# Cross-attention stages L2 and L3: value blocks ahead of the masked scores, the bias row in the first tile's step, key bias and exp table first

## The chip, the cores and the metric

The kernel is one program on one core of a Trainium2 chip. The core has five engines with one instruction stream each: PE (TensorE, matrix products and transposes), DVE (VectorE), ACT (ScalarE), POOL (GpSimd) and SP, which here only issues transfers. Each engine works through its own stream in order and waits at semaphores. ACT also issues transfers from its stream. The time is that of one execution on the device in microseconds, and lower is better.

## The reference

An input `x` of 4 x 1024 x 256 goes through four layers. Each layer adds a gated cross-attention to a short context (4 x 77 x 256) and then a gated feed-forward block. The change concerns the attentions of the third and fourth layer (L2 and L3 in the names), which one function builds. Both are ordinary softmax attentions with 16 heads of 16; L2 has an additive mask and no biases, L3 a key mask and biases on q, k, v and the output.

```python
q = (x_q @ Wq.T).reshape(b, tq, h, hd).transpose(0, 2, 1, 3)
k = (x_kv @ Wk.T).reshape(b, tk, h, hd).transpose(0, 2, 1, 3)
v = (x_kv @ Wv.T).reshape(b, tk, h, hd).transpose(0, 2, 1, 3)
scores = jnp.einsum('bhqd,bhkd->bhqk', q, k) / jnp.sqrt(jnp.float32(hd))
scores = scores + attn_mask
...
w = jax.nn.softmax(scores, axis=-1)
out = jnp.einsum('bhqk,bhkd->bhqd', w, v)
...
x = x + jnp.tanh(g_xattn[2]) * _L2_xattn_ref(_layernorm(x, axis=-1), ctx_1024, ...)
x = x + jnp.tanh(g_xattn[3]) * _L3_xattn_ref(_layernorm(x, axis=-1), ctx_1024, ctx_1024, ...)
```

## The kernel before

The program is eight stages in a row, one for each attention and each feed-forward block. A barrier of all engines closes every stage, so nothing of the next one, its transfers included, starts earlier. `x` stays in the on-chip memory (`all_x`) as 32 tiles of 128 rows by 256; 8 tiles belong to one batch element.

`stage_mha` builds the L2 attention (names `l2x_...`) and the L3 attention (`l3x_...`). The context part comes first: PE projects the 4 x 77 context rows with `wk` into `score` (`project`, L2078), ACT copies the result to `kt` with the key bias `bk` (L2210), and DVE multiplies `kt` with the head mask `hm` into block-diagonal keys `kbd` (`key_block`, L1926). Values go the same way: `project` with `wv` into `p_bank`, ACT copy to `vt` (L2231), DVE `value_block` into `vbd` (L1955), then PE turns `vbd` (`first_values`, L2089), and ACT copies it to `vrow` (L2222). For the output bias PE multiplies `bvb` (the value bias, spread over 128 columns, L1951) with `wo` (`out_bias`, L2119), and DVE makes the row `brow` from it in two instructions (L1995, L1996).

A tile t then runs through: DVE `norm` (`xn`, L170); PE `turn` (L2126); ACT `copy_x`; PE `query` (L2135); ACT `copy_q` (`qt`, L2252); PE `scores` (L2148); DVE `masked_scores` (L2013), and for each half of the heads a maximum and a subtraction (`shift`, L2022 and L2024); ACT `exps` (L2264); PE `values`, which transposes the probabilities (L2164), while ACT copies them to `pt` (`copy_p`, L2272), and multiplies them with `vrow` (L2179); DVE `scale_o` (L2030, L2033); PE `turn_o` and `output` (L2193); DVE `update` of `x` and its statistics.

`unrolled(n, parts)` writes the order of every engine out: in step s, each part in the list handles tile s + lead, if there is one. The order in the list is the order in the stream. So a list entry that does something for tile 0 alone (`first_keys`, `first_values`, `out_bias`, `values_projection`) stands at one fixed place, in the step -lead. In `values`, the product with `vrow` waits for `v_ready` (all of `vrow`) and, in tile 0, for `brow_ready`, because the bias product stands in the same `o_bank` until DVE has read it. The Vector stream first waits for one semaphore, `bias_loaded`, up to 64, so for all four bias transfers, before it scales `bk`.

## Time and profile before

| | us |
|---|---|
| median of 3 runs | 2046.88 |
| lowest and highest of the 3 | 2042.46, 2048.35 |
| the profiled execution, its own time | 2042.43 |
| its span in the profile | 2040.7 |
| L2 attention, from its first transfer to the next stage's | 872.95 to 1135.24 |
| L3 attention, its first transfer | 1561.14 |

The profile's span covers nearly the whole execution: 1.7 us lie around it. Of the busy time PE has 1697.1 us (83% of the span), DVE 1152.6 (56%), ACT 887.5 (43%) and POOL 325.0 (16%). The rows further down give a start in us from the span's start, a duration, the engine and the line; a bracket at the end is the time that the engine sat idle before it, and who ended that.

### The profile page before, as it was taken

How to read it: one execution, taken by the hardware profiler on the slowest of the kernel's cores; microseconds unless marked ns; L12 is line 12 of the kernel's file. 1: busy time of each engine (PE TensorE's matmuls, PEld its weight loads, DVE VectorE, ACT ScalarE, POOL GpSimd, SP SyncE). 2: the span in 40 equal slices, each digit the busy share in tenths (PEclk: the TensorE clock that was granted, in tenths of full speed). 3: DMA queues.
4: the chain of work that ended last, by engine and by line, in shares of the span. 5: the costliest groups of instructions: out<-in, count | busy, mean ns of one | idle time of the engine just before them, and what ended most of it. 6: DMA issues, size and time to landing. Idle time of an engine off the chain costs nothing. (4 is left out here: it accounts for less than half of the span.)

```text
span 2040.7 us, 30775 instructions
## 1 busy us (share of the span) xinstructions
PE 1697.1 (83%) x10297; PEld 1295.8 (63%) x10297; DVE 1152.6 (56%) x2517; ACT 887.5 (43%) x1828; POOL 325.0 (16%) x362
## 2 busy tenths in 40 slices
PE   6888478888669999779999839999982899969998
PEld 4444234555456666558888729999971788855446
DVE  4544546776534556769998472322227798861115
ACT  2222356766343220236665235565543566633223
POOL 1000000000000000411110044555545111101110
PEclk8888789999789999889999659999996999989999
DMA  4000100000300000010000751222225000010002
...
DMA packets 63458, 78.53 MB, mean 38 GB/s; under 512 B 13999, under 2 KB 53195, under 8 KB 62936
## 3 DMA queue, kind: packets, MB, share of 16 engines
...
## 5 line engine op out<-in xcount | busy, mean ns | idle before, releaser
L2635 PEld LDWEIGHTS moe_bank<-moe_xt,moe_w1e 128*128 128x128 f32 x1264 | 155.0, 194 | 5.9 <-DVE moe_xt L2493 1.9
L2635 PE MATMUL moe_bank<-moe_xt,moe_w1e 128*128 128x128 f32 x1264 | 155.8, 277 | 1.1 <-DVE moe_xt L2493 1.1
L2645 PE MATMUL moe_bank<-moe_w,moe_xin 128*128 x632 | 149.3, 379 | 0.0
L2696 ACT ACTIVATE moe_xin<-moe_bank,moe_b 128x128 f32<-128x128 f32 x316 | 90.3, 368 | 125.1 <-PE moe_bank L2635 125.1
L356 PE MATMUL l0f_hb<-l0f_xt,l0f_w 128*128 128x512 f32 x256 | 123.5, 613 | 5.6 <-DVE l0f_a L287 3.9
L935 POOL TENSOR_TENSOR all_x<-all_x,l1f_bias 128x256 f32 x32 | 23.1, 726 | 647.6 <-DVE l1f_xn L170 647.6
L2645 PEld LDWEIGHTS moe_bank<-moe_w,moe_xin 128*128 128x128 f32 x632 | 114.0, 190 | 12.3
L175 DVE BATCH_NORM_STATS2 all_stats<-all_x 128x6 f32<-128x256 f32 (+1 forms) x256 | 105.8, 422 | 15.3 <-DMA all_x<-in_x 2.9
L2502 DVE TENSOR_TENSOR moe_y<-moe_bank,moe_b2r 128x256 f32<-128x256 f32 x79 | 33.5, 424 | 118.8 <-PE moe_bank L2645 118.8
L2562 POOL DMA_INDIRECT moe_results<-moe_y,moe_row x79 | 78.1, 989 | 125.0 <-DVE moe_y L2502 121.7
L2493 DVE COPY moe_xt<-moe_bank 128x256 f32<-128x256 f32 x79 | 33.5, 425 | 106.7 <-PE moe_bank L2623 106.7
L1749 PE MATMUL l3f_bank<-l3f_xt,l3f_wx 128*128 128x512 f32 x192 | 86.4, 600 | 0.0
L2687 ACT ACTIVATE moe_w1e<-moe_w 128x1024 f32 x79 | 83.5, 1058 | 3.3 <-issue 1.5
L2179 PE MATMUL l2x_o_bank<-l2x_vrow,l2x_pt 128*128 128x136 f32 (+1 forms) x640 | 82.3, 284 | 2.9 <-DVE l2x_brow L1996 2.9
L2179 PE MATMUL l3x_o_bank<-l3x_vrow,l3x_pt 128*128 128x136 f32 (+1 forms) x640 | 82.3, 284 | 2.9 <-DVE l3x_brow L1996 2.9
L1824 ACT ACTIVATE l3f_gate<-l3f_bank,l3f_bg 128x512 f32<-128x512 f32 x48 | 32.9, 687 | 115.1 <-PE l3f_bank L1757 105.4
L2557 POOL DMA_INDIRECT moe_xin<-moe_inputs,moe_token x79 | 76.9, 974 | 26.3 <-PE moe_bank L2623 21.6
L2179 PEld LDWEIGHTS l2x_o_bank<-l2x_vrow,l2x_pt 128*128 128x128 f32 (+1 forms) x640 | 78.1, 193 | 3.6 <-issue 3.1
L2179 PEld LDWEIGHTS l3x_o_bank<-l3x_vrow,l3x_pt 128*128 128x128 f32 (+1 forms) x640 | 78.1, 193 | 3.6 <-issue 3.1
L285 DVE SCALAR_TENSOR_TENSOR l0f_a<-l0f_hb,l0f_cw,l0f_a 128x1023 f32<-128x1023 f32 x32 | 41.0, 1283 | 61.5 <-ACT l0f_a L467 61.5
L356 PEld LDWEIGHTS l0f_hb<-l0f_xt,l0f_w 128*128 128x128 f32 x256 | 45.8, 196 | 46.9 <-issue 45.9
L1757 PE MATMUL l3f_bank<-l3f_ct,l3f_wc 128*128 128x512 f32 x144 | 63.8, 592 | 0.0
...
## 6 DMA issues: line engine op xcount, KB each, us to landing
...
```

Source lines behind the costliest of these rows:

```text
L175: return nc.vector.bn_stats(sh.stats[:, ds(t * 6, 6)], x_tile(sh, t))
L285: k.link(nc.vector.scalar_tensor_tensor(a[:, u, 1:S], h[:, 0:S - 1], cw[:, m, 0:1], a[:, u, 1:S], ALU.mult, ALU.add))
L356: ins = nc.tensor.matmul(hb[g % 2][:, half * 512:(half + 1) * 512], w1[:, d, m * P:(m + 1) * P], xt[:, b % 2, d, half * 512:(half + 1) * 5 ...
L1749: ins = nc.tensor.matmul(bank[3 * m + k][:, :], wx[:, k, c, m * P:(m + 1) * P], xt[:, c, b * S + j * G:b * S + (j + 1) * G], start=(c == 0 ...
L1757: ins = nc.tensor.matmul(bank[3 * m + k][:, :], wc[:, k, c, m * P:(m + 1) * P], ct[:, b % 2, c, j * G:(j + 1) * G], start=False, stop=(c = ...
L2179: ins = nc.tensor.matmul(o_bank[:, m * VW:(m + 1) * VW], pt[0:rows(i), u, n, j * P:(j + 1) * P], vrow[0:rows(i), ds((t // TB) * (DC * NV * ...
L2557: nc.gpsimd.indirect_dma_start(out=gathered(t), out_offset=None, in_=xnd, in_offset=bass.IndirectOffsetOnAxis(ap=token[:, t:t + 1], axis=0 ...
L2562: nc.gpsimd.indirect_dma_start(out=ys, out_offset=bass.IndirectOffsetOnAxis(ap=row[:, t:t + 1], axis=0), in_=y[:, u, :], in_offset=None).t ...
L2635: ins = nc.tensor.matmul(out, w1e[:, at:at + P], xt[:, u, c * P:(c + 1) * P], start=(c == 0), stop=(c == DC - 1))
L2645: ins = nc.tensor.matmul(bank[4 + u][:, 0:D], ht[:, u, c * P:(c + 1) * P], w2[:, ds(e * (HC * D) + c * D, D)], start=(c == 0), stop=(c == ...
L2687: nc.scalar.activation(w1e[:, u * DC * HID:(u + 1) * DC * HID], w1[:, ds(e * (DC * HID), DC * HID)], ACT.Copy).then_inc(s.w1e_ready, 1)
L2696: ins = nc.scalar.activation(ht[:, u, m * P:(m + 1) * P], bank[1 + u][:, m * P:(m + 1) * P], ACT.Gelu, bias=b1[:, ds(e * HC + m, 1)])
```

## The change

`unrolled` gets another order in three lists. On DVE `first_values` now stands ahead of `masked_scores`, and `out_bias` has lead 2 in place of 1, so it comes in the step in which tile 0 gets its scores, one step earlier. On PE `out_bias` and `first_values` change places. On ACT `first_values` comes ahead of both `exps`. The copy to `bvb` moves behind the first keys and the mask. The transfers that ACT issues get another order, with a semaphore of their own for the key bias (`bk_loaded`) and for the output bias (`bo_loaded`): key bias, head mask, `wv`, query and value bias, `wo`, output bias. A new activation with Exp on one column (`warm`) follows them, whose result nobody reads.

```diff
--- before.py
+++ after.py
@@ -1889,6 +1889,7 @@
         vbd = s.sb("vbd", [P, 2, DC, HW_])
         vrow = s.sb("vrow", [P, B * DC * NV * VW])
         ones_row = s.sb("ones_row", [P, NV, HH])
+        warm = s.sb("warm", [P, 1])
         keyrow = s.sb("keyrow", [P, B, SK], U8)
         mraw = s.sb("mraw", [P, TB, SK], U8 if masked else F32)
         mask_t = s.sb("mask_t", [P, T, SK])
@@ -1904,7 +1905,7 @@
         x_bank, o_bank = s.ps("x_bank", [P, 512]), s.ps("o_bank", [P, 512])
         score = s.ps("score", [P, NG, 512])
         p_bank = [s.ps(f"p_bank{k}", [P, 512]) for k in range(2)]
-        sems = ["wk_loaded", "wv_loaded", "wq_loaded", "wo_loaded", "hm_loaded", "bias_loaded", "small_loaded", "kv_ps", "kv_ready", "vbd_ready", "kbd_ready", "kbd_rest_ready", "v_ps", "v_ready", "brow_ps",
+        sems = ["wk_loaded", "wv_loaded", "wq_loaded", "wo_loaded", "hm_loaded", "bk_loaded", "bias_loaded", "bo_loaded", "small_loaded", "kv_ps", "kv_ready", "vbd_ready", "kbd_ready", "kbd_rest_ready", "v_ps", "v_ready", "brow_ps",
                 "brow_ready", "bvb_ready", "bk_ready", "set_step", "mask_set", "xn_ready", "xt_ps", "xt_ready", "q_ps", "q_ready",
                 "s_ps", "added", "max_ready", "shifted", "exp_ready", "ones_set", "inv_ready", "pt_ps", "pt_ready",
                 "o_ps", "o_ready", "ot_ps", "ot_ready", "y_ps", "biased", "x_ready", "stats_ready"]
@@ -1942,13 +1943,12 @@
             def _(dve):
                 c = norm_vector(nc, dve, sh, s)
                 if bias_names:
-                    dve.wait_ge(s.bias_loaded, 64)
+                    dve.wait_ge(s.bk_loaded, 16)
                 else:
                     for a in (bq, bk, bv):
                         c.link(nc.vector.memset(a[:, :], 0.0))
                     c.link(nc.vector.memset(brow[:, :], 0.0))
                 nc.vector.tensor_scalar(bk[:, :], bk[:, :], HD ** -0.5, None, ALU.mult).then_inc(s.bk_ready, 1)
-                nc.vector.tensor_copy(bvb[:, :, :], bv[:, :].unsqueeze(2).to_broadcast((P, DC, P))).then_inc(s.bvb_ready, 1)
                 hmb = hm[:, :].unsqueeze(2).to_broadcast((P, HH, SK))
 
                 def value_block(b, k):
@@ -1972,6 +1972,9 @@
                             key_block(nc.vector, 0, k, s.kbd_ready)
                         dve.wait_ge(s.small_loaded, smalls)
                         mask_block(0)
+                        if bias_names:
+                            dve.wait_ge(s.bias_loaded, 32)
+                        nc.vector.tensor_copy(bvb[:, :, :], bv[:, :].unsqueeze(2).to_broadcast((P, DC, P))).then_inc(s.bvb_ready, 1)
 
                 def first_values(t, u):
                     if t == 0:
@@ -1991,6 +1994,8 @@
                 def out_bias(t, u):
                     if t:
                         return
+                    if bias_names:
+                        dve.wait_ge(s.bo_loaded, 16)
                     dve.wait_ge(s.brow_ps, 1)
                     c.link(nc.vector.tensor_tensor(brow[:, :], o_bank[:, 0:D], brow[:, :], ALU.add))
                     nc.vector.tensor_scalar(brow[:, :], brow[:, :], tg, None, ALU.mult).then_inc(s.brow_ready, 1)
@@ -2042,8 +2047,8 @@
                     dve.wait_ge(s.x_ready, ev(t))
                     tile_stats(nc, sh, t).then_inc(s.stats_ready, 1)
 
-                unrolled(T, [(scale_o, 0), (norm, 4), (first_keys, 3), (masked_scores, 2), (shift(0), 2), (update, 0), (shift(1), 2), (first_values, 2),
-                             (out_bias, 1), (context, 0)])
+                unrolled(T, [(scale_o, 0), (norm, 4), (first_keys, 3), (first_values, 2), (masked_scores, 2), (shift(0), 2), (update, 0), (shift(1), 2),
+                             (out_bias, 2), (context, 0)])
                 dve.wait_ge(s.stats_ready, T)
 
             @block.gpsimd
@@ -2193,17 +2198,21 @@
                         ins = nc.tensor.matmul(o_bank[:, 0:D], ot[:, u, k * P:(k + 1) * P], wo[:, k, :], start=(k == 0), stop=(k == DC - 1))
                     ins.then_inc(s.y_ps, 1)
 
-                unrolled(T, [(turn, 3), (scores, 2), (turn_o, 0), (query, 3), (output, 0), (values_projection, 3), (first_values, 2), (out_bias, 2), (values, 1), (context, 0)])
+                unrolled(T, [(turn, 3), (scores, 2), (turn_o, 0), (query, 3), (output, 0), (values_projection, 3), (out_bias, 2), (first_values, 2), (values, 1), (context, 0)])
 
             @block.scalar
             def _(act):
+                if bias_names:
+                    act.dma_start(bk[:, :], io[bias_names[1]]).then_inc(s.bk_loaded, 16)
                 act.dma_start(hm[:, :], io.head_mask).then_inc(s.hm_loaded, 16)
+                act.dma_start(wv[:, :, :], weight_view(io[wv_T])).then_inc(s.wv_loaded, 16)
                 if bias_names:
-                    for a, n in zip((bq, bk, bv), bias_names):
+                    for a, n in ((bq, bias_names[0]), (bv, bias_names[2])):
                         act.dma_start(a[:, :], io[n]).then_inc(s.bias_loaded, 16)
-                    act.dma_start(brow[:, :], io[bias_names[3]].partition_broadcast(P)).then_inc(s.bias_loaded, 16)
-                act.dma_start(wv[:, :, :], weight_view(io[wv_T])).then_inc(s.wv_loaded, 16)
                 act.dma_start(wo[:, :, :], weight_view(io[wo_T])).then_inc(s.wo_loaded, 16)
+                if bias_names:
+                    act.dma_start(brow[:, :], io[bias_names[3]].partition_broadcast(P)).then_inc(s.bo_loaded, 16)
+                nc.scalar.activation(warm[:, :], sh.gates[:, 0:1], ACT.Exp)
                 act.wait_ge(s.bk_ready, 1)
                 for j in range(DC):
                     act.wait_ge(s.kv_ps, j + 1)
@@ -2246,6 +2255,8 @@
                     nc.scalar.activation(xt[:, u, :], x_bank[:, 0:D], ACT.Copy).then_inc(s.xt_ready, 1)
 
                 def copy_q(t, u):
+                    if t == 0 and bias_names:
+                        act.wait_ge(s.bias_loaded, 32)
                     act.wait_ge(s.q_ps, ev(t))
                     act.wait_ge(s.s_ps, ev(t, back=2))
                     for m in range(DC):
@@ -2271,7 +2282,7 @@
                         act.wait_ge(s.pt_ps, ev(t, NB, n + 1))
                         nc.scalar.activation(pt[0:r, u, n, 0:k * P], p_bank[n % 2][0:r, 0:k * P], ACT.Copy).then_inc(s.pt_ready, 1)
 
-                unrolled(T, [(copy_x, 3), (copy_o, 0), (copy_q, 3), (values_projection, 3), (copy_p, 1), (exps(0), 2), (exps(1), 2), (first_values, 2), (context, 0)])
+                unrolled(T, [(copy_x, 3), (copy_o, 0), (copy_q, 3), (values_projection, 3), (copy_p, 1), (first_values, 2), (exps(0), 2), (exps(1), 2), (context, 0)])
 
 
 def stage_l2_xattn(nc, io, sh):
```

On PE in the L3 attention (L2 reads alike), from the query of tile 1 on, to the product with `vrow` in tile 0. The first fence is before, the second the same place after the change.

```order
L2135 MATMUL l3x_x_bank<-l3x_xt,l3x_wq 128x128 x4
L2089 MATMUL l3x_p_bank<-all_ident,l3x_vbd 128x128 x8
L2089 MATMUL l3x_p_bank<-all_ident,l3x_vbd 104x128 x2
L2119 MATMUL l3x_o_bank<-l3x_wo,l3x_bvb 128x256 x2
L2126 MATMUL l3x_x_bank<-all_ident,l3x_xn 128x128 x2
L2148 MATMUL l3x_score<-l3x_kbd,l3x_qt 128x154 x8
L2135 MATMUL l3x_x_bank<-l3x_xt,l3x_wq 128x128 x4
L2164 MATMUL l3x_p_bank<-all_ident,l3x_pr 128x128 x8
```

```order
L2140 MATMUL l3x_x_bank<-l3x_xt,l3x_wq 128x128 x4
L2124 MATMUL l3x_o_bank<-l3x_wo,l3x_bvb 128x256 x2
L2094 MATMUL l3x_p_bank<-all_ident,l3x_vbd 128x128 x8
L2094 MATMUL l3x_p_bank<-all_ident,l3x_vbd 104x128 x2
L2131 MATMUL l3x_x_bank<-all_ident,l3x_xn 128x128 x2
L2153 MATMUL l3x_score<-l3x_kbd,l3x_qt 128x154 x8
L2140 MATMUL l3x_x_bank<-l3x_xt,l3x_wq 128x128 x4
L2169 MATMUL l3x_p_bank<-all_ident,l3x_pr 128x128 x8
```

The bias product (`l3x_o_bank<-l3x_wo,l3x_bvb`) went from behind the transposes of `vbd` to ahead of them. The number of instructions is the same.

On DVE in the L3 attention, from the first keys on, before and after; `l3x_vbd` are the value blocks, `l3x_pr` the masked scores.

```order
L170 TENSOR_SCALAR l3x_xn<-all_x,all_rstd,all_shift 128x256
L2013 TENSOR_TENSOR l3x_pr<-l3x_score,l3x_mask_t 128x616 x2
L2022 TENSOR_REDUCE l3x_mx<-l3x_pr 128x8
L2024 TENSOR_TENSOR l3x_pr<-l3x_pr,l3x_mx 128x616
L2022 TENSOR_REDUCE l3x_mx<-l3x_pr 128x8
L2024 TENSOR_TENSOR l3x_pr<-l3x_pr,l3x_mx 128x616
L1955 TENSOR_TENSOR l3x_vbd<-l3x_vt,l3x_hm 128x616 x2
L170 TENSOR_SCALAR l3x_xn<-all_x,all_rstd,all_shift 128x256
L2013 TENSOR_TENSOR l3x_pr<-l3x_score,l3x_mask_t 128x616 x2
L2022 TENSOR_REDUCE l3x_mx<-l3x_pr 128x8
L2024 TENSOR_TENSOR l3x_pr<-l3x_pr,l3x_mx 128x616
L2022 TENSOR_REDUCE l3x_mx<-l3x_pr 128x8
```

```order
L170 TENSOR_SCALAR l3x_xn<-all_x,all_rstd,all_shift 128x256
L1955 TENSOR_TENSOR l3x_vbd<-l3x_vt,l3x_hm 128x616 x2
L2018 TENSOR_TENSOR l3x_pr<-l3x_score,l3x_mask_t 128x616 x2
L2027 TENSOR_REDUCE l3x_mx<-l3x_pr 128x8
L2029 TENSOR_TENSOR l3x_pr<-l3x_pr,l3x_mx 128x616
L2027 TENSOR_REDUCE l3x_mx<-l3x_pr 128x8
L2029 TENSOR_TENSOR l3x_pr<-l3x_pr,l3x_mx 128x616
L2000 TENSOR_TENSOR l3x_brow<-l3x_o_bank,l3x_brow 128x256
L2001 TENSOR_SCALAR l3x_brow<-l3x_brow,all_gates 128x256
L170 TENSOR_SCALAR l3x_xn<-all_x,all_rstd,all_shift 128x256
L2018 TENSOR_TENSOR l3x_pr<-l3x_score,l3x_mask_t 128x616 x2
L2027 TENSOR_REDUCE l3x_mx<-l3x_pr 128x8
```

The two value blocks moved ahead of the first masked scores, and `brow`, which before followed the second tile's subtractions, now stands between the first tile's and the second tile's.

On ACT at the start of the L3 attention, before and after.

```order
L2200 DMA l3x_hm<-in_head_mask 128x8
L2203 DMA l3x_bq<-in_L_xattn_b_q_cols 128x2
L2203 DMA l3x_bk<-in_L_xattn_b_k_cols 128x2
L2203 DMA l3x_bv<-in_L_xattn_b_v_cols 128x2
L2204 DMA l3x_brow<-in_L_xattn_b_o 128x256
L2205 DMA l3x_wv<-in_L_xattn_W_v_T 128x2x256
L2206 DMA l3x_wo<-in_L_xattn_W_o_T 128x2x256
L2210 ACTIVATE l3x_kt<-l3x_score,l3x_bk 128x308 x2
L2246 ACTIVATE l3x_xt<-l3x_x_bank 128x256
L2252 ACTIVATE l3x_qt<-l3x_x_bank,l3x_bq 128x128 x2
L2231 ACTIVATE l3x_vt<-l3x_p_bank 128x308 x2
```

```order
L2206 DMA l3x_bk<-in_L_xattn_b_k_cols 128x2
L2207 DMA l3x_hm<-in_head_mask 128x8
L2208 DMA l3x_wv<-in_L_xattn_W_v_T 128x2x256
L2211 DMA l3x_bq<-in_L_xattn_b_q_cols 128x2
L2211 DMA l3x_bv<-in_L_xattn_b_v_cols 128x2
L2212 DMA l3x_wo<-in_L_xattn_W_o_T 128x2x256
L2214 DMA l3x_brow<-in_L_xattn_b_o 128x256
L2215 ACT_TABLE_LOAD
L2215 ACTIVATE l3x_warm<-all_gates 128x1
L2219 ACTIVATE l3x_kt<-l3x_score,l3x_bk 128x308 x2
L2255 ACTIVATE l3x_xt<-l3x_x_bank 128x256
```

The key bias is the first transfer in place of the third, `wv` the third in place of the sixth, the output bias the last. The table load, which before stood ahead of the first exps, comes with `warm` ahead of the first `kt` copy.

## Rows read from the trace of the kernel before

**Rows 1.** Busy time by stretch: PE, PEld, DVE, ACT, POOL, then PEclk, DMA share, GB/s

```profile
884.00:896.00 12.00, 6.91 (x44) 5.24 (x42) 6.25 (x9) 4.67 (x10) 0.00 (x0) 0.73 0.00 1
...
920.00:950.00 30.00, 28.39 (x264) 25.58 (x264) 27.59 (x48) 18.43 (x40) 4.09 (x5) 1.00 0.01 1
```

**Rows 2.** Timeline of the L2 attention, its first tile

```profile
884.37 0.43 ACT L2231 ACTIVATE l2x_vt<-l2x_p_bank 128x308 f32<-128x308 f32 x1 [0.61 <-PE l2x_p_bank L2078]
885.22 1.16 PE L2135 MATMUL l2x_x_bank<-l2x_xt,l2x_wq 128*128 128x128 f32 x8
885.42 1.51 DVE L2013 TENSOR_TENSOR l2x_pr<-l2x_score,l2x_mask_t 128x616 f32<-128x616 f32 x2 [2.22 <-PE l2x_score L2148]
...
889.20 0.80 DVE L2024 TENSOR_TENSOR l2x_pr<-l2x_pr,l2x_mx 128x616 f32<-128x616 f32 x1
889.92 1.50 DVE L1955 TENSOR_TENSOR l2x_vbd<-l2x_vt,l2x_hm 128x616 f32<-128x616 f32 x2
...
891.47 2.56 PE L2089 MATMUL l2x_p_bank<-all_ident,l2x_vbd 128*128 128x128 f32 x10 [5.09 <-DVE l2x_vbd L1955]
892.63 0.69 ACT L2222 ACTIVATE l2x_vrow<-l2x_p_bank,all_gates 128x512 f32<-128x512 f32 x1 [1.88 <-PE l2x_p_bank L2089]
...
893.48 1.22 ACT L2222 ACTIVATE l2x_vrow<-l2x_p_bank,all_gates 128x512 f32<-128x512 f32 x3 [0.17 <-PE l2x_p_bank L2089]
...
895.54 0.63 PE L2126 MATMUL l2x_x_bank<-all_ident,l2x_xn 128*128 128x128 f32 x2
...
897.14 1.51 DVE L2013 TENSOR_TENSOR l2x_pr<-l2x_score,l2x_mask_t 128x616 f32<-128x616 f32 x2 [5.40 <-PE l2x_score L2148]
...
901.64 0.42 DVE L1995 TENSOR_TENSOR l2x_brow<-l2x_o_bank,l2x_brow 128x256 f32<-128x256 f32 x1
...
902.70 4.22 PE L2179 MATMUL l2x_o_bank<-l2x_vrow,l2x_pt 128*128 128x136 f32 x20 [2.92 <-DVE l2x_brow L1996]
...
906.96 0.26 DVE L2030 RECIPROCAL l2x_ri<-l2x_o_bank 128x16 f32<-128x16 f32 x1 [4.51 <-PE l2x_o_bank L2179]
```

**Rows 3.** Timeline of the L2 attention: durations and distances at the full clock

```profile
896.93 1.16 PE L2135 MATMUL l2x_x_bank<-l2x_xt,l2x_wq 128*128 128x128 f32 x8
...
897.92 1.04 PE L2164 MATMUL l2x_p_bank<-all_ident,l2x_pr 128*128 128x128 f32 x8
...
898.64 1.56 ACT L2272 ACTIVATE l2x_pt<-l2x_p_bank 128x512 f32<-128x512 f32 x3
...
908.98 1.03 PE L2193 MATMUL l2x_o_bank<-l2x_wo,l2x_ot 128*128 128x256 f32 x4
...
911.52 2.52 PE L2179 MATMUL l2x_o_bank<-l2x_vrow,l2x_pt 128*128 128x136 f32 x20
```

**Rows 4.** Timeline, the L2 and then the L3 attention's start

```profile
880.22 0.41 PE L2126 MATMUL l2x_x_bank<-all_ident,l2x_xn 128*128 128x128 f32 x2 [0.28 <-ACTq L2213]
...
1564.06 4.48 PE L2078 MATMUL l3x_score<-all_ctx_t,l3x_wk 128*128 128x308 f32 x8 [43.55 <-DMA l3x_wk<-in_L_xattn_W_k_T]
...
1567.88 0.33 DVE L1950 TENSOR_SCALAR l3x_bk<-l3x_bk 128x2 f32<-128x2 f32 x1 [2.64 <-DMA l3x_brow<-in_L_xattn_b_o]
...
1568.24 0.93 ACT L2210 ACTIVATE l3x_kt<-l3x_score,l3x_bk 128x308 f32<-128x308 f32 x2 [17.66 <-DVE l3x_bk L1950]
...
1569.44 0.44 PE L2126 MATMUL l3x_x_bank<-all_ident,l3x_xn 128*128 128x128 f32 x2 [0.91 <-DVE l3x_xn L170]
...
1576.32 1.28 ACT L2264 ACT_TABLE_LOAD   x1
...
1577.75 0.72 ACT L2264 ACTIVATE l3x_pr<-l3x_pr 128x616 f32<-128x616 f32 x1 [0.15 <-DVE l3x_pr L2024]
```

**Rows 5.** DMA issues at the L3 start: KB each, median us to landing

```profile
l3x_wo<-in_L_xattn_W_o_T ACTq DMA_DIRECT2D x1, 256.0 KB, 4.9
...
l3x_bk<-in_L_xattn_b_k_cols ACTq DMA_DIRECT2D x1, 1.0 KB, 3.7
```

**Rows 6.** Timeline, DVE: the reciprocal of tile 1, L2

```profile
914.07 0.26 DVE L2030 RECIPROCAL l2x_ri<-l2x_o_bank 128x16 f32<-128x16 f32 x1 [0.69 <-PE l2x_o_bank L2179]
```

## The prediction

> **What bounds the kernel now.** I first read the busy time by stretch, to see whether the two attentions are full. In mid-stage they are: PE is busy 28.39 of 30 us and DVE 27.59, at the full clock of 2.4 GHz [rows 1]. Their first tile is not: PE has 6.91 of 12 us, and the mean granted clock is 0.73 of full, so about half of this stretch ran at 1.2 GHz. The timeline of the L2 attention says why [rows 2]. After the query of tile 1 ends at 886.38, PE stands at the transposes of the value blocks, 5.09 us, because DVE makes these blocks only after tile 0's masked scores, maxima and subtractions. Behind the transposes in PE's stream stand the bias product, the transposes of tile 2's `xn` (895.54) and the scores of tile 1, so DVE then waits 5.40 us for these scores. Last, PE waits 2.92 us for `brow`, which DVE makes after tile 1's subtractions, and DVE waits 4.51 us for the product with `vrow`, which runs at the low clock in 4.22 us. From there the pace is even: the reciprocals of tiles 0 and 1 start at 906.96 and 914.07, 7.11 us apart [rows 2, 6], and the engines keep to this cycle. What shifts the first reciprocal shifts the rest of the stage and, since barriers separate the stages, the end. That is the place where I read the change off: the start of tile 0's reciprocal, in each of the two stages.
>
> **L2, step by step.** The last `vt` copy ends at 884.37 + 0.43 = 884.80, and DVE, idle 2.22 us there, can start the value blocks at about 884.9 [rows 2]. They take 1.50 us (1.42 to the next start, 889.92 to 891.34 by the pair's own overlap), so the blocks are ready at 886.4 and tile 0's masked scores start at 886.3 instead of 885.42: 0.9 us later. From that start to the end of the last subtraction takes 889.20 + 0.80 - 885.42 = 4.58 us, which gives 890.9. `brow` is two instructions, the first of 0.42 us; the product that waits for both began 902.70 - 901.64 = 1.06 us after the first. I take 0.8, to 891.7, the next `xn` 0.4, so DVE is free for tile 1's masked scores at 892.1.
>
> PE: the query of tile 1 ends at 886.38 [rows 2]. The bias product follows at once; at the full clock its shape takes 1.03 us (the row of L2193, 908.98) [rows 3], with overlap to 887.3. The value blocks are ready, so their transposes start there. For the same ten transposes of probabilities ACT's copy starts 0.72 us after PE's (898.64 against 897.92) [rows 3]. ACT then copies `vrow` in 0.69 + 1.22 = 1.9 us [rows 2], 888.0 to 890.0. PE's transposes are done at 889.1, and tile 2's turn and tile 1's scores, which took no more than 897.14 - 895.54 = 1.6 us at partly the low clock, at about 890.2. So tile 1's masked scores start when DVE is free, 892.1, not 897.14, and its last subtraction ends at 896.7.
>
> ACT: the exps now stand behind the `vrow` copies. The first, whose subtraction is done at about 889.3, waits to 890.0 for them; the second starts at 890.9, when its subtraction is done, and ends at 891.6. Behind it stands the copy of tile 2's `xt`, which the query of tile 2 waits for: query at 892.1. From query to the transposes is 0.99 us, from there to the last of the copies to `pt` 2.3 us (898.64 + 1.56 - 897.92), but in the even cycle the product starts 1.7 us after the transposes, so I put it at 2.7 us after the query, 894.8 [rows 3]. `brow` is ready three us before, so that wait is gone. With the product at the full clock, 2.52 us [rows 3], the reciprocal starts at 897.4: 906.96 - 897.4 = 9.6 us gained.
>
> **L3** has the same rows 688.7 to 689.4 us later, so the same 9.6, and three edits more. DVE there waits 2.64 us for the last of the four bias transfers, the copy to `bvb` follows, and tile 0's first turn starts at 1569.44, 0.90 us after the projection's end at 1564.06 + 4.48 = 1568.54. In L2, where no bias is loaded, PE idled 0.28 us there [rows 4]. The key bias landed 3.7 us after its issue [rows 5]; issued first, at about 1561.15, it is there at 1564.9, before DVE's norm is done (1567.88 - 2.64 = 1565.24), and PE's projection, which it doesn't need, is the bound: gain 0.6, taken as 0.5 because `wv` now loads beside `wk`. The bounds of this edit are 0 and 0.6 us. Second, the Exp table load, 1.28 us [rows 4]. Before it lay under DVE's maxima (after the load, ACT still idled 0.15 us for DVE's subtraction before the first exps at 1577.75), so its removal there gives nothing; its new place is under PE's projection, where ACT idled 17.66 us. In L2 `warm` falls under the projection as well; without that cover it would cost less than the 0.43 us of a copy of 308 columns [rows 2], and in L3 1.28 more. Third, `wo`, which PE now wants ahead of the value transposes, and behind which the whole PE stream would stand: it is needed at about 1575 and, issued near 1563.7 with 4.9 us to landing [rows 5], there at 1569. The output bias is issued behind it and used on DVE near 1580. Nothing for both.
>
> **The clock.** The sum so far is 9.6 + 9.6 + 0.5 = 19.7 us. It presupposes PE at 2.4 GHz, and the new order leaves an idle gap: from 890.2 to 892.1, 1.9 us. In the rows the clock fell after PE idled 5.09 us and again after 2.92 us, where the product took 4.22 us in place of 2.52; in the even cycle it stays, with 30 - 28.39 = 1.6 us of idling over four tiles, so 0.4 us for each [rows 1 to 3]. A gap of 1.9 lies between 0.4 and 2.92, nearer to 2.92 (1.0 against 1.5), so I take the low clock for one stretch: 4.22 - 2.52 = 1.7 us, in each stage. The bounds are 0 and, with the transposes slow as well (ten in 2.56 us against eight in 1.04, so 1.3 for ten), 2.9. The Trainium skill, "TensorE: Matmul & The Clock Gate", section "Why this matters for your kernels", asks for no idle gaps over about 3 us between bursts; by this rule alone the gap of 1.9 us would cost nothing and the sum would be 19.7. The row of 2.92 us, just under that figure, shows a fall, so the rule is not sharp enough here.
>
> **Sum.** 19.7 - 3.4 = 16.3 us off the profiled execution's 2042.4: 2026.1. That execution is as fast as the fastest of the three runs; the median lies 4.4 above. I put the expected median 2 us above the sum: 2028. A measurement of this kernel tells 0.3%, some 6 us, from no change.
>
> **Rivals.** *The clock holds* (0.27): the gap is short enough, as the skill's rule has it. Full 19.7 us, 2022.7; for it speaks that PE is busy nearly without a gap from 880 to 890, against it the fall after 2.92 us.
> *The first tile takes the gain back in part* (0.12): ACT's copies before the exps or the slow transposes delay tile 0 more than I count, and both stages lose 2.9 us to the clock, so that with 2 us of such delay about 5 us each remain: 2042.4 - 10 = 2032. For it: ACT's exps do wait 0.7 us. Against: DVE is the later one in the sum.
> *It is hidden anyway* (0.04): tile 1 gains, but the even cycle is reached at the old time, because something outside these rows sets it (the x update, POOL). 2042. Against it: the rows show no such wait, and POOL is nearly idle.
> *Slower* (0.02): PE falls to the low clock in the new gap and, with DVE now feeding it sooner but in small pieces, stays there. At the low clock the product costs 1.7 and the transposes 1.2 us more per tile; from four tiles on (4 x 2.9 = 11.6 us in a stage) the gain of 9.6 is gone, and at seven in each stage it is 2 x (20.3 - 9.6) = 21 us slower: 2063. Against it: after each fall in the rows a tile of solid work brought the full clock back.
> My forecast, the low clock for one stretch in each stage, has 0.55.
>
> **Numbers.** The two first cases span 2022.7 to 2026.1 for a run like the profiled one, up to 2033 with the 4.4 us of the median and the third case 2032 to 2036. The range 2020 to 2035 leaves out the last two cases, part of the third, and a tail below. Faster by over 0.3%: the first three cases, 0.94; within: 0.04; slower: 0.02.
>
> **What would show it.** In the changed profile, in L2: value blocks on DVE from about 884.9, the bias product on PE right after the query at 886.4, PE's 5.09 us wait and DVE's 5.40 us wait gone, tile 1's masked scores near 892.1, tile 0's reciprocal near 897 to 899, and then 7.11 us between reciprocals as before. In L3: the scaling of `bk` right behind the norm, the table load under the projection. PEclk in the second twelve us tells forecast from rival. The prediction is wrong if DVE waits for PE's scores of tile 1 again, if the product with `vrow` still waits for `brow`, or if the later distance between tiles grows.

## The result and the profile after

| | before | changed |
|---|---|---|
| median, us | 2047.22 (4 runs, 2042.46 to 2048.35) | 2029.75 (4 runs, 2027.91 to 2032.66) |
| ratio | | 0.992, 95% interval 0.9899 to 0.9942 |
| profiled execution, us | 2042.43 | 2031.57 |
| L2 attention, first transfer to the next stage's | 262.29 | 253.78 |
| L3 attention, the same | 263.34 | 254.08 |
| the six other stages together | 1515.07 | 1521.94 |

The change is faster by 17.5 us of the medians, well over the 6 us that a measurement tells; forecast were 2028 us and a range of 2020 to 2035. The two attentions gave 8.51 + 9.26 = 17.77 us. The two profiled executions differ by only 10.9 us, because the six stages that the change does not touch took 6.9 us longer in the second one. Of these, 2.65 us lie in the stage between the two attentions, and that part comes with the change (next section). The page of the changed kernel has the shorter span and nearly the same busy times as before: the gain is idle time.

```profile
span 2029.8 us, 30778 instructions
...
PE 1697.8 (84%) x10297; PEld 1296.2 (64%) x10297; DVE 1153.8 (57%) x2517; ACT 887.8 (44%) x1830; POOL 325.4 (16%) x362
```

The stage lengths come from the first transfer of each stage, since a barrier stands ahead of it. These are those of the changed kernel, from its timeline of issues: 1130.00 - 876.22 = 253.78 for L2, 1812.63 - 1558.55 = 254.08 for L3.

```profile
876.22 0.38 SPq L1933 DMA_DIRECT2D l2x_wk<-in_L_xattn_Wk_T  x1
...
1130.00 0.37 SPq L2386 DMA_DIRECT2D moe_wr<-in_L_ffn_Wr  x1
...
1558.55 0.37 SPq L1933 DMA_DIRECT2D l3x_wk<-in_L_xattn_W_k_T  x1
...
1812.63 0.37 SPq L1637 DMA_DIRECT2D l3f_wx<-in_L_ffn_wf_T  x1
```

The L2 attention's first tile in the changed kernel, its timeline, to be read against [rows 2] (the stage began 3.27 us later in this execution, so subtract that):

```profile
888.08 1.51 DVE L1955 TENSOR_TENSOR l2x_vbd<-l2x_vt,l2x_hm 128x616 f32<-128x616 f32 x2 [1.23 <-ACT l2x_vt L2240]
...
889.46 1.03 PE L2124 MATMUL l2x_o_bank<-l2x_wo,l2x_bvb 128*128 128x256 f32 x4
889.50 1.50 DVE L2018 TENSOR_TENSOR l2x_pr<-l2x_score,l2x_mask_t 128x616 f32<-128x616 f32 x2
...
890.33 1.04 PE L2094 MATMUL l2x_p_bank<-all_ident,l2x_vbd 128*128 128x128 f32 x8
...
894.00 0.42 DVE L2000 TENSOR_TENSOR l2x_brow<-l2x_o_bank,l2x_brow 128x256 f32<-128x256 f32 x1
...
895.04 1.50 DVE L2018 TENSOR_TENSOR l2x_pr<-l2x_score,l2x_mask_t 128x616 f32<-128x616 f32 x2
895.15 1.17 PE L2140 MATMUL l2x_x_bank<-l2x_xt,l2x_wq 128*128 128x128 f32 x8 [2.07 <-ACT l2x_xt L2255]
...
896.15 2.50 PE L2169 MATMUL l2x_p_bank<-all_ident,l2x_pr 128*128 128x128 f32 x10
...
898.45 3.07 PE L2184 MATMUL l2x_o_bank<-l2x_vrow,l2x_pt 128*128 128x136 f32 x20
...
901.55 0.26 DVE L2035 RECIPROCAL l2x_ri<-l2x_o_bank 128x16 f32<-128x16 f32 x1 [1.58 <-PE l2x_o_bank L2184]
...
908.66 0.26 DVE L2035 RECIPROCAL l2x_ri<-l2x_o_bank 128x16 f32<-128x16 f32 x1 [0.69 <-PE l2x_o_bank L2184]
```

PE's wait of 5.09 us for the value blocks, DVE's of 5.40 us for the scores and PE's of 2.92 us for `brow` are gone: the masked scores of tile 1 and the product with `vrow` carry no bracket. New is PE's gap of 2.07 us ahead of the query of tile 2, which waits for ACT's copy to `xt`. The ten transposes behind it take 2.50 us, as at the low clock. The reciprocals of tiles 0 and 1 are 7.11 us apart, as in [rows 2, 6].

The table of busy times, with columns as in [rows 1]; the first number behind POOL's is PEclk, the granted clock as a share of 2.4 GHz:

```profile
887.27:899.27 12.00, 9.59 (x82) 7.91 (x81) 11.02 (x17) 7.16 (x17) 2.88 (x4) 0.87 0.01 1
...
923.27:953.27 30.00, 28.39 (x273) 25.27 (x271) 26.22 (x47) 18.82 (x41) 4.09 (x5) 1.00 0.01 1
...
894.00:896.00 2.00, 0.84 (x7) 0.85 (x8) 1.97 (x6) 0.99 (x2) 1.12 (x2) 1.00 0.00 0
896.00:899.00 3.00, 3.00 (x16) 2.56 (x16) 2.97 (x4) 2.13 (x6) 1.77 (x3) 0.53 0.00 0
```

In the 12 us that answer to the first row of [rows 1], PE is busy 9.59 us in place of 6.91 and DVE 11.02 in place of 6.25. The even cycle is unchanged (PE 28.39 of 30 both times). The clock falls right behind the gap: 1.00, then 0.53 (nearly all at 1.2 GHz).

### The profile page after: what moved, and what is told of

The parts are those of the page before. It is cut to its first block and busy times, and to the rows that moved or that the text cites. A ratio compares the mean times of both kernels' runs of the same rounds, so it can differ in the third digit from the quotient of the medians.

```text
span 2029.8 us, 30778 instructions
## 1 busy us (share of the span) xinstructions
PE 1697.8 (84%) x10297; PEld 1296.2 (64%) x10297; DVE 1153.8 (57%) x2517; ACT 887.8 (44%) x1830; POOL 325.4 (16%) x362
```

## The experiments

All times in this table run from the first transfer of the stage, so they can be compared between executions whose earlier stages differ. "Reciprocal" is the start of tile 0's, L2 then L3.

| kernel | median, us | ratio (95%) | L2 length | L3 length | reciprocal |
|---|---|---|---|---|---|
| before | 2047.22 | | 262.29 | 263.34 | 34.01, 35.19 |
| changed | 2029.75 | 0.992 (0.9899-0.9942) | 253.78 | 254.08 | 25.33, 25.85 |
| e1_orders | 2033.65 | 0.993 (0.9907-0.9953) | 253.74 | 257.24 | 25.40, 29.00 |
| e2_loads | 2046.11 | 0.9999 (0.9985-1.0012) | 262.33 | 263.31 | 33.98, 35.09 |
| e3_values_only | 2035.82 | 0.9945 (0.9924-0.9967) | 256.19 | 256.64 | 27.74, 28.40 |
| e4_brow_only | 2032.92 | 0.994 (0.9917-0.9963) | 256.70 | 256.97 | 28.35, 28.73 |
| e5_act_late | 2030.44 | 0.9926 (0.9906-0.9946) | 255.79 | 256.46 | 27.46, 28.21 |
| e6_x_early | 2026.21 | 0.9907 (0.9889-0.9924) | 252.26 | 252.53 | 23.64, 24.19 |
| e7_filler | 2024.16, one run | | 252.68 | 253.19 | 24.32, 24.93 |
| e8_orders_warm | 2031.53, one run | | 253.69 | 255.36 | 25.36, 27.14 |
| e9_no_warm | 2030.68, one run | | 253.55 | 254.36 | 25.21, 26.16 |
| e10_before_again | 2048.88, one run | | 262.34 | 263.29 | 34.03, 35.09 |
| e11_orders_again | 2031.67, one run | | 253.76 | 255.43 | 25.44, 27.23 |

The medians of the kernel before beside these were 2045.68 (e1 to e4) and 2046.20 (e5 to e8); one run of it beside e9 to e11 took 2040.42. The six other stages, which no kernel here touches, sum to 1515 us in one profiled execution of the kernel before and to 1521 in the other (e10). A few us between two medians can be that alone, so I read the stage lengths.

One of the six stages is not free of the change, though its code is. The MoE feed-forward between the two attentions, from its first transfer to that of L3, takes 428.2 to 429.1 us in five profiles (changed, e1, e8, e9, e11) and 425.7 to 426.6 in the eight others, those of the kernel before, e6 and e7 among them. The timelines of the two, at the same distance of 92.4 us into this stage, the kernel before first, then the changed kernel:

```profile
1227.66 2.05 PE L2635 MATMUL moe_bank<-moe_xt,moe_w1e 128*128 128x128 f32 x16 [0.52 <-DVE moe_xt L2493]
```

```profile
1222.44 3.78 PE L2646 MATMUL moe_bank<-moe_xt,moe_w1e 128*128 128x128 f32 x16 [0.52 <-DVE moe_xt L2504]
```

The same 16 products take 1.7 us more, since the clock rises to full later: its mean is 0.98 in the 6 us from 1227.24 before, and 0.56 in the 6 us from 1222.00 in the changed kernel. So some 2.6 us of the 17.77 are lost again behind L2. Why is not shown; a fall of the clock in L2 is not enough, since e3_values_only has one and takes 425.9 us here.

**e1_orders: the three new lists alone.** The kernel before with the orders of the change; transfers, the copy to `bvb` and the table load stay where they were.

```diff
# DVE
-... (first_keys, 3), (masked_scores, 2), ..., (shift(1), 2), (first_values, 2), (out_bias, 1), (context, 0)
+... (first_keys, 3), (first_values, 2), (masked_scores, 2), ..., (shift(1), 2), (out_bias, 2), (context, 0)
# PE
-... (first_values, 2), (out_bias, 2), (values, 1), (context, 0)
+... (out_bias, 2), (first_values, 2), (values, 1), (context, 0)
# ACT
-... (exps(0), 2), (exps(1), 2), (first_values, 2), (context, 0)
+... (first_values, 2), (exps(0), 2), (exps(1), 2), (context, 0)
```

> The three reordered lists alone; transfers, the wait for all four biases, the early copy to bvb and no warm activation, as before. Measure: from a stage's first transfer to tile 0's reciprocal, 34.0 us (L2) and 35.2 us (L3) before, 25.3 and 25.9 in the changed kernel. My theory (the orders are the whole gain of L2, and in L3 all but the late key bias and the exposed table load): L2 25.3; L3 25.9 + 0.5 for the key bias + 0.6, since the table load of 1.28 us now stands between the vrow copies and exps that DVE releases 0.7 us later, so about 27.0. Both stages together 16.5 us shorter than before. Rival (transfers and warm matter for more, as the table load is now fully on the path): L3 28 or later. Rival (they are worth nothing): L3 25.9.

L2 takes 253.74 us, as in the changed kernel (253.78): the orders are all of L2's gain. L3 takes 257.24, which is 3.16 us more than in the changed kernel; 1.1 were expected (27.0 against 25.9 to the reciprocal), and the prediction had 0.5 for the loads. The timeline of L3 in e1_orders:

```profile
1568.09 0.17 DVE L1950 TENSOR_SCALAR l3x_bk<-l3x_bk 128x2 f32<-128x2 f32 x1 [3.07 <-DMA l3x_brow<-in_L_xattn_b_o]
...
1569.66 0.44 PE L2126 MATMUL l3x_x_bank<-all_ident,l3x_xn 128*128 128x128 f32 x2 [1.87 <-DVE l3x_xn L170]
...
1570.57 2.08 PE L2135 MATMUL l3x_x_bank<-l3x_xt,l3x_wq 128*128 128x128 f32 x8 [0.47 <-ACT l3x_xt L2246]
...
1572.44 2.93 PE L2078 MATMUL l3x_p_bank<-all_ctx_t,l3x_wv 128*128 128x308 f32 x8
...
1580.60 1.28 ACT L2264 ACT_TABLE_LOAD   x1
```

DVE waits for the last of four bias transfers, and PE stands 1.87 us behind that. The query and the value projection behind this gap take 2.08 and 2.93 us, where the changed kernel has 1.16 and 2.24: PE runs at the low clock there (windows of e1_orders, PEclk 0.57).

```profile
1570.00:1574.00 4.00, 3.53 (x13) 2.97 (x13) 2.06 (x4) 1.01 (x3) 0.00 (x0) 0.57 0.00 0
```

The 3.16 us are there when the query of tile 2 starts (22.63 us into L3 against 19.47): 0.98 at the first turn (8.75 against 7.77), 1.58 from there to tile 0's masked scores (16.38 against 13.82), and 0.60 from these to the query, where the table load is now on ACT's path. Whether the 1.58 are the orders' doing or chance, e10 and e11 were made for.

**e2_loads: everything but the three lists.** The changed kernel with the old lists (the diff of e1_orders read backwards).

> The transfers' order, the wait for the key bias alone, the later copy to bvb and the warm activation; the three lists as before. My theory: L2 as before (34.0 us to the first reciprocal), L3 0.5 us earlier (34.7), total within noise of before. Rival (the loads carry a good part of the gain): more than 2 us in L3.

Ratio 0.9999; L3 263.31 against 263.34, and the first turn 8.29 us into the stage (before 8.30). The loads alone gave nothing in this profile, where 0.5 us had been expected in L3. The timelines of the L3 start show what they move, e2_loads first:

```profile
1569.26 0.37 SPq L1933 DMA_DIRECT2D l3x_wk<-in_L_xattn_W_k_T  x1
...
1572.65 4.34 PE L2083 MATMUL l3x_score<-all_ctx_t,l3x_wk 128*128 128x308 f32 x8 [44.09 <-DMA l3x_wk<-in_L_xattn_W_k_T]
...
1577.55 0.41 PE L2131 MATMUL l3x_x_bank<-all_ident,l3x_xn 128*128 128x128 f32 x2 [0.56 <-ACTq L2222]
```

and the changed kernel (its first transfer is at 1558.55, shown above):

```profile
1561.71 4.04 PE L2083 MATMUL l3x_score<-all_ctx_t,l3x_wk 128*128 128x308 f32 x8 [44.12 <-DMA l3x_wk<-in_L_xattn_W_k_T]
...
1562.19 1.28 ACT L2215 ACT_TABLE_LOAD   x1 [13.77 <-issue]
...
1566.32 0.41 PE L2131 MATMUL l3x_x_bank<-all_ident,l3x_xn 128*128 128x128 f32 x2 [0.57 <-ACTq L2222]
```

The wait for the biases has gone; PE idles 0.56 us at the turn in place of 0.91. On the other side `wk` lands later in the kernels that issue `wv` close behind it: the projection starts 3.39 us after the first transfer in e2_loads (1572.65 - 1569.26) and 3.16 in the changed kernel, before 2.92 (1564.06 - 1561.14 [rows 4]). The projection itself takes 3.8 to 4.5 us, as the clock happens to rise in it. So one profile doesn't settle a term of 0.5 us. Over all profiles it stands like this: with the new loads and the early table load (seven kernels) the first turn starts 7.73 to 8.29 us into L3, mean 7.93, and `wk` is there after 3.16 to 3.39; with the old transfers (five profiles) 8.30 to 8.75, mean 8.43, and 2.89 to 3.08. The loads bring the turn forward by 0.5 us in the mean, and e2_loads is the poorest of the seven.

**e3_values_only: value blocks first, bias row as before.**

```diff
 # DVE
-(out_bias, 2), (context, 0)
+(out_bias, 1), (context, 0)
 # PE
-(out_bias, 2), (first_values, 2)
+(first_values, 2), (out_bias, 2)
```

> As the changed kernel, but the bias product and its row stay where they were before (PE behind the value transposes, DVE behind tile 1's subtractions). My theory: PE's 5.1 us wait is gone, tile 1's masked scores start at about 18 us after the stage's first transfer, but the product with vrow then waits for the row, which DVE makes at about 22.6 to 23.4: first reciprocal at about 26.2 us (L2), so 7.8 us of the 8.7 gained. Rival A (the value blocks are all of it): 25.3, as in the changed kernel. Rival B (the row is the larger part): 29 or later.

L2 is 6.10 us shorter than before, L3 6.70. Tile 1's masked scores start 18.05 us into L2 in place of 24.19, so the earlier start of these scores, 6.14 us, is all of it. The reciprocal comes at 27.74, not at the 26.2 expected: the product still waits for `brow`, which DVE makes behind tile 1's subtractions, and it runs at the low clock, in 4.10 us, which the expectation had not counted. PE's query of tile 2 already stands 1.83 us for ACT's copy (timeline, L2):

```profile
898.99 1.16 PE L2140 MATMUL l2x_x_bank<-l2x_xt,l2x_wq 128*128 128x128 f32 x8 [1.83 <-ACT l2x_xt L2255]
...
902.65 0.42 DVE L2000 TENSOR_TENSOR l2x_brow<-l2x_o_bank,l2x_brow 128x256 f32<-128x256 f32 x1
...
903.71 4.10 PE L2184 MATMUL l2x_o_bank<-l2x_vrow,l2x_pt 128*128 128x136 f32 x20 [1.24 <-DVE l2x_brow L2001]
...
907.85 0.26 DVE L2035 RECIPROCAL l2x_ri<-l2x_o_bank 128x16 f32<-128x16 f32 x1 [4.39 <-PE l2x_o_bank L2184]
```

**e4_brow_only: bias row first, value blocks as before.**

```diff
 # DVE
-(first_values, 2), (masked_scores, 2), (shift(0), 2), (update, 0), (shift(1), 2), (out_bias, 2)
+(masked_scores, 2), (shift(0), 2), (update, 0), (shift(1), 2), (first_values, 2), (out_bias, 2)
 # ACT
-(first_values, 2), (exps(0), 2), (exps(1), 2)
+(exps(0), 2), (exps(1), 2), (first_values, 2)
```

> As the changed kernel, but the value blocks stay behind the first tile's subtractions on DVE, and the vrow copies behind the exps on ACT; only the bias product and its row are early. My theory: PE still waits about 4.2 us for the value blocks, tile 1's masked scores start near 22.4 us, the product no longer waits for the row: first reciprocal at 28 to 29.5 us in L2, 5.3 us gained, so that the two parts overlap (7.8 + 5.3 against 8.7). Rival (the parts add up): 34.0 - 0.9 = 33.1.

L2 is 5.59 us shorter than before, L3 6.37. PE still stands 4.23 us for the value blocks, and the product follows at the full clock, in 2.56 us and without a wait (timeline, L2):

```profile
889.81 2.56 PE L2094 MATMUL l2x_p_bank<-all_ident,l2x_vbd 128*128 128x128 f32 x10 [4.23 <-DVE l2x_vbd L1955]
...
897.00 2.56 PE L2184 MATMUL l2x_o_bank<-l2x_vrow,l2x_pt 128*128 128x136 f32 x20
```

The parts account for it: 2.92 us of wait for `brow` [rows 2], 4.22 - 2.56 = 1.66 us of clock in the product, and 24.19 - 23.03 = 1.16 us by which tile 1's masked scores come earlier, since the bias product no longer stands ahead of them in PE's stream: 5.7. Alone the two parts give 6.10 and 5.59 in L2; together they give 8.51, not 11.7. On top of e3_values_only the early row moves the reciprocal by 2.4 us (27.74 to 25.33) and not by 5.7, for three reasons. The wait for `brow` is 1.24 us there and not 2.92, since PE's query of tile 2 comes later than tile 1's masked scores, behind ACT's copy. The product goes from 4.10 to 3.07 us and not to 2.56, since the clock falls again in the full change (e7 below). And the 1.16 us in PE's stream are worth nothing where DVE is the later one: tile 1's masked scores carry no bracket in the changed kernel. That `brow` between the tiles delays these scores (18.82 against 18.05) costs nothing, since the query of tile 2 starts at 18.93 and 18.88.

**e5_act_late: ACT's list as before.** DVE and PE as changed, `first_values` behind both exps on ACT.

> As the changed kernel, but ACT copies vrow behind tile 0's exps, as before the change. My theory (ACT's place matters, since PE's last value transposes wait for the first of these copies, and tile 2's turn and tile 1's scores stand behind them): PE idles about 4 us, query of tile 2 at 20.9 us after the first transfer in place of 18.9, clock low, first reciprocal at 27.5 to 28.5 us in L2 (25.3 in the changed kernel), each stage 2 to 3 us longer. Rival (exps ahead help, because they gate tile 0): 25 or earlier.

L2 is 2.01 us longer than in the changed kernel, L3 2.38. The copies to `vrow` now stand behind exps that wait for DVE's second subtraction, PE stands 4.10 us in the middle of the value transposes, and tile 2's turn and tile 1's scores stand behind them (timeline, L2):

```profile
894.49 0.43 PE L2094 MATMUL l2x_p_bank<-all_ident,l2x_vbd 128*104 128x128 f32 x2 [4.10 <-ACT l2x_vrow L2231]
...
896.40 2.08 PE L2140 MATMUL l2x_x_bank<-l2x_xt,l2x_wq 128*128 128x128 f32 x8
```

So the third list is a part of the gain, and DVE's and PE's new places need it.

**e6_x_early: the copy to tile 2's `xt` between the two exps.** In the changed kernel this copy stands behind the second exp, and the query of tile 2 waits for it.

```diff
+                def next_x(t, u):
+                    if t == 0:
+                        copy_x(2, 0)
+
+                def later_x(t, u):
+                    if t != 2:
+                        copy_x(t, u)
+
-(copy_x, 3), ... (first_values, 2), (exps(0), 2), (exps(1), 2), (context, 0)
+(later_x, 3), ... (first_values, 2), (exps(0), 2), (next_x, 2), (exps(1), 2), (context, 0)
```

> As the changed kernel, but ACT's copy of tile 2's transposed xn stands between tile 0's two exps, where ACT idles 0.7 us for DVE, so that PE's query of tile 2 and the transposes behind it start 1.3 us earlier and PE's idle gap falls from 2.07 to about 0.8 us. My theory (the product of tile 0 waits for the chain exps, copy, query, transposes, and the gap lowers the clock): product at 20.6 at the full clock, first reciprocal at 23.4 to 23.5, now bounded by DVE's subtractions of tile 1; each stage 1.9 us shorter than in the changed kernel. Rival (DVE already bounds it): reciprocal no earlier than 25. Rival (the clock falls all the same): 24.3.

PE's gap shrinks from 2.07 to 0.64 us (timeline, L2), the clock stays (windows, PEclk 1.00 in the stretch behind it), and the product takes 2.56 us:

```profile
894.13 1.16 PE L2140 MATMUL l2x_x_bank<-l2x_xt,l2x_wq 128*128 128x128 f32 x8 [0.64 <-ACT l2x_xt L2255]
...
896.82 2.56 PE L2184 MATMUL l2x_o_bank<-l2x_vrow,l2x_pt 128*128 128x136 f32 x20
```

```profile
894.00:897.00 3.00, 2.44 (x19) 2.18 (x20) 2.96 (x7) 2.40 (x6) 1.71 (x3) 1.00 0.00 0
```

The reciprocal, at 23.64 where 23.4 to 23.5 was expected, carries no bracket, so DVE's own work bounds it now. The stages are 1.52 and 1.55 us shorter than in the changed kernel, where 1.9 was expected. The median is 3.5 us lower, the lowest of the kernels with more than one run; the MoE stage, 2.00 us shorter in this profile than in the changed one, may have a part in that. Against the kernel before it is 0.9907. The intervals of this ratio and the changed kernel's overlap; that it is the better of the two rests on the stage lengths.

**e7_filler: work for PE in the gap.** The bias product a second and third time, into a bank that is free then, ahead of the place where PE would stand. Nobody reads the result.

```diff
+                def filler(t, u):
+                    if t:
+                        return
+                    pe.wait_ge(s.v_ready, NB)
+                    for _ in range(2):
+                        for k in range(DC):
+                            nc.tensor.matmul(p_bank[1][:, 0:D], bvb[:, k, :], wo[:, k, :], start=(k == 0), stop=(k == DC - 1))
+
-(turn, 3), (scores, 2), (turn_o, 0), ...
+(turn, 3), (scores, 2), (filler, 1), (turn_o, 0), ...
```

> As the changed kernel, with two more bias products of PE into a bank that nobody reads then, placed in PE's idle gap between tile 1's scores and tile 2's query (extra work, no result used). My theory (the gap of 2.07 us lowers the clock): the gap is 0.2 us, PEclk stays at full, the product takes 2.52 us in place of 3.07 and the transposes before it 1.44 in place of 2.5, first reciprocal at 23.9 to 24.2 us in L2 (25.3). Rival (the fall has another cause): PEclk falls in the same place, 25.3 us or later.

The query of tile 2 starts at the same distance into L2 as in the changed kernel (19.03 us, 18.93 there), since it still waits for `xt`. But the clock is full behind it, and from query to reciprocal it takes 899.00 - 893.71 = 5.29 us in place of 901.55 - 895.15 = 6.40 (timeline and windows, L2):

```profile
893.71 1.16 PE L2140 MATMUL l2x_x_bank<-l2x_xt,l2x_wq 128*128 128x128 f32 x8
...
896.40 2.56 PE L2184 MATMUL l2x_o_bank<-l2x_vrow,l2x_pt 128*128 128x136 f32 x20
...
899.00 0.26 DVE L2035 RECIPROCAL l2x_ri<-l2x_o_bank 128x16 f32<-128x16 f32 x1 [0.47 <-PE l2x_o_bank L2184]
```

```profile
894.00:897.00 3.00, 2.58 (x23) 2.31 (x23) 2.96 (x5) 1.98 (x5) 2.34 (x4) 1.00 0.00 0
```

What differs is that PE works for 1.99 us where it had idled 2.07, and the clock stays full in both stages, as it does in both stages of e6_x_early. So it is PE's idling there that lowers the clock. The fall costs 1.1 us in L2 (253.78 - 252.68) and 0.9 in L3 by the stage lengths, and 1.1 in both from query to reciprocal.

**e8_orders_warm: e1_orders with the table load early.** It loads the table under the projection, as the change does, and leaves the transfers as before.

```diff
+                nc.scalar.activation(warm[:, :], sh.gates[:, 0:1], ACT.Exp)
                 act.wait_ge(s.bk_ready, 1)
```

> The three reordered lists and the warm activation, but the biases loaded and waited for as before. The orders alone gave 29.0 us to the first reciprocal in L3, the changed kernel 25.9: 3.1 us lie in the loads. My theory: 0.7 of them are the exposed table load, 0.6 to 1 the late turn of tile 0, and the rest PE at the low clock because it idled for the key bias. So here 28.3 if the clock falls at the start again, 26.6 if it does not. Rival (the table load is the whole loss): 25.9.

L3 takes 255.36 us, 1.88 less than e1_orders. From tile 0's masked scores to the query of tile 2 it takes 5.65 us in place of 6.25: 0.6 us are the load's. The reciprocal follows the query by 5.28 us in place of 6.37, so 1.1 are the clock's, which did not fall here behind the same gap of 2.07 us (timeline and windows, L3):

```profile
1579.55 1.16 PE L2136 MATMUL l3x_x_bank<-l3x_xt,l3x_wq 128*128 128x128 f32 x8 [2.07 <-ACT l3x_xt L2248]
...
1582.23 2.56 PE L2180 MATMUL l3x_o_bank<-l3x_vrow,l3x_pt 128*128 128x136 f32 x20
```

```profile
1578.00:1581.00 3.00, 1.46 (x13) 1.46 (x14) 2.96 (x7) 1.25 (x3) 1.73 (x3) 1.00 0.00 0
```

The reciprocal comes at 27.14, between the 28.3 expected with a fall at the start and the 26.6 without: the fall at the start came, the later one did not. The 1.28 us to the changed kernel are the later turn (8.45 against 7.77, 0.7 us) and again a low clock behind the wait for the biases (PE idles 1.28 us at the turn; the first query and the value projection take 1.27 and 3.85 us in place of 1.16 and 2.24, together 1.7), less the 1.1 us of clock that this execution saved at the query of tile 2.

**e9_no_warm: the changed kernel without `warm`.** The complement of e8: early transfers, late table load.

```diff
-                nc.scalar.activation(warm[:, :], sh.gates[:, 0:1], ACT.Exp)
```

> The changed kernel without the early table load; the complement of e8_orders_warm. If the late biases cost L3 through the clock (theory), the first query of L3 takes 1.16 us and its projection of values 2.24 us here as in the changed kernel, and only the load is exposed: L3 0.6 us longer than the changed kernel, 254.7. If orders and loads interact in another way (rival), L3 is 255.4 or more with the clock full at that place. L2 as changed, 253.7, or up to 0.6 more if its load is exposed too (the table of L2 may be loaded already).

L3 takes 254.36 us, only 0.3 more than the changed kernel. The timeline of L3 has both sides of the early load:

```profile
1565.14 0.41 PE L2130 MATMUL l3x_x_bank<-all_ident,l3x_xn 128*128 128x128 f32 x2 [0.28 <-ACTq L2220]
...
1577.47 1.69 PE L2139 MATMUL l3x_x_bank<-l3x_xt,l3x_wq 128*128 128x128 f32 x8 [2.67 <-ACT l3x_xt L2253]
```

Without it PE idles 0.28 us at the first turn, as in L2, and not 0.57; at the query of tile 2 it idles 2.67 us, and not 2.07. So the early load costs 0.3 us at the stage's start and saves 0.6 later. How it costs them stays open: ACT's `kt` copies start at the same distances in both (5.7 and 7.2 us), and what the turn waits for are ACT's semaphore increments, which stand behind them in the program. In L2, where `warm` runs but no table is loaded, the turn waits 0.28.

**e10_before_again and e11_orders_again: the kernel before and e1_orders once more.**

> The kernel before once more, to see whether the clock behind PE's wait for the biases in L3 (0.91 us there in its first profile, with the full clock behind it) falls in some executions of the same code. Theory, that it is chance of the execution: L3's first query at 1.2 to 2.1 us and the value projection up to 3.9 us in place of 2.24, stage up to 1.7 us longer than 263.34. Rival, that the old orders hold the clock there: query 1.16, projection 2.24, 263.3 again.

> The same code as e1_orders once more, where L3 took 257.24 with PE's gap of 1.87 us ahead of the first turn and a low clock behind it (query 2.08, value projection 2.93). Theory, that the fall there is chance: L3 between 255.5 (no fall) and 257.3 (fall). Rival, that the orders and the late biases together always cost it: 257.2 again.

The kernel before repeats itself, as the rival had it: L3 263.29, a gap of 0.84 us at the first turn, full clock behind it. e11 does not repeat e1: the same code takes 255.43 us in place of 257.24. The timeline of e11, L3:

```profile
1566.23 0.44 PE L2126 MATMUL l3x_x_bank<-all_ident,l3x_xn 128*128 128x128 f32 x2 [1.06 <-DVE l3x_xn L170]
...
1567.14 1.16 PE L2135 MATMUL l3x_x_bank<-l3x_xt,l3x_wq 128*128 128x128 f32 x8 [0.47 <-ACT l3x_xt L2246]
```

The gap is 1.06 us, the query takes 1.16. So the 1.6 us of e1's low clock come and go with the execution. The gap does so too: in e1 the projection ended 0.36 us earlier (it took 3.83 us in place of 4.31) and the turn came 0.44 us later, so these two profiles do not show another clock behind the same gap. With the late biases the gap was 0.84, 0.91 and 1.06 us with the full clock behind it, and 1.28 and 1.87 with a fall; in all eight profiles with the early biases it was 0.28 to 0.57, and no fall. What is left between e11 and the changed kernel, 1.35 us, is 0.54 at the turn, 0.60 for the table load and 0.2 behind the query.

## Why the prediction was right, and where not

**What bounds, and where to read the change off: right.** The three waits of [rows 2] are gone, the distance of the reciprocals is still 7.11 us, and the stage's gain equals the shift of tile 0's reciprocal: 34.01 - 25.33 = 8.7 against 8.5 us of length in L2, 9.3 against 9.3 in L3.

**The first tile's sum at the full clock (9.6): right.** e7_filler, the change with the clock held, gained 262.29 - 252.68 = 9.61 us in L2, and 263.34 - 253.19 = 10.15 in L3, where 9.6 + 0.5 = 10.1 was the sum. The steps of the sum stand beside the changed profile like this, in us from L2's first transfer:

| step | predicted | measured |
|---|---|---|
| value blocks start | 884.9 - 872.95 = 11.95 | 11.86 |
| tile 0 masked scores | 13.35 | 13.28 |
| value transposes | 14.35 | 14.11 |
| tile 1 masked scores | 19.15 | 18.82 |
| query of tile 2 | 19.15 | 18.93 |
| product, low clock before it not counted | 21.85 | 22.23 (e7: 21.72) |
| reciprocal, with the clock term | 26.15 | 25.33 |

One duration on DVE was off: the subtraction that follows the gap takes 1.15 us in place of 0.80 (last section). Tile 0's product did not wait for it.

**The clock: mechanism right, size off.** I took one stretch of low clock in each stage, 1.7 us by the product's 4.22 - 2.52. It fell in both stages, and cost 1.1 us (6.40 against 5.29 from query to reciprocal). The transposes of the probabilities ran at the low clock too, but part of that lay beside ACT's copies to `pt`, for which PE stands 0.42 us even at the full clock (e7); the product started 0.5 us later for it (22.23 against 21.72) and had only part of its columns at the low clock (3.07 us, and 2.86 in L3). In my sum the product bore all of the fall and the transposes none. The fall came earlier than that, and the clock was back within the product.

The Trainium skill, "TensorE: Matmul & The Clock Gate", section "Why this matters for your kernels", asks for no idle gaps over about 3 us between bursts. Here the granted clock fell behind a gap of 2.07 us in both stages of the changed kernel and in the L2 stages of e1, e8, e9 and e11 (2.06 in two of them), and it stayed behind the same gap in e8's L3. At the same place it fell behind 1.83 us in both stages of e3 and behind 2.67 us in the L3 of e1, e9 and e11. So the rule is too lax for this case, and the length of a gap does not decide by itself. What differs in e8's L3 I have not tried.

**The rival "the clock holds" (0.27)** would have given 9.6 us in each stage; it did not happen, but it was only 1.1 us a stage away, which no median of this kernel could tell. **"The first tile takes the gain back in part" (0.12):** not seen, but e5_act_late shows how near it was: with ACT's old order 2.0 to 2.4 us of each stage are lost. **The two others** were not seen: the pace behind tile 0 is as before.

**The key bias (0.5 us in L3): right in the mean, and not the whole of it.** L3's first turn came 0.53 us earlier, and 0.5 over all profiles; `wk` lands 0.1 to 0.5 us later, and the turn then waits 0.57 us, where I had expected L2's 0.28 (with the early table load; e9). What I had not seen is that the late biases open a gap on PE that lowers the clock in some executions: in two of five profiles, for 1.6 to 1.7 us. None of that shows in the two profiles of the kernel before, so it is no part of the difference that I forecast. How much of it is in e1's median is not known: one of its five runs was profiled. My bounds for the edit, 0 and 0.6, hold for the turn alone.

**The table load, "its removal there gives nothing": right for the sum, wrong for what `warm` is worth.** Against the kernel before it gives nothing: the load was hidden there, and in the change it is hidden again. But it was read where the load stood before, under DVE's maxima. With `first_values` ahead of the exps, ACT has the copies to `vrow` to do in just that time, so the load comes on the path with 0.6 us of its 1.28. It is the cover that the change itself takes away. And the new place is not free: 0.3 us at the first turn, though ACT had idled 17.66 us ahead of that copy [rows 4], for a reason that I have not found. The net is 0.3 us against the change without `warm` (e9, one profile each), and none of it is in the difference to the kernel before. On `wo` and the output bias "nothing for both" held: neither the value transposes nor `brow` waited for a transfer.

**The sum.** 16.3 us predicted, 17.77 measured in the two stages. The clock's size is 0.6 of the difference in each stage. The other 0.25 lie in L3, which gained 0.75 us more than L2 and not 0.5: 0.50 are the turn, 0.15 come from the first profile of the kernel before, where tile 1's masked scores were 1.18 us later in L3 than in L2 but the turn only 1.03 (1.07 and 1.05 in e10), and 0.09 lie behind the reciprocal. That the median came within 1.8 us of 2028 is in part luck. The profiled execution of the kernel before lay 4.8 us under its median, and I had added 2; the larger gain in the stages made up for 1.5 us of that, and the later clock in the MoE stage, which I had not looked for, worked against it.
